# Cumulative sums of dt in a Mamba-2 block on TensorE: eight fp32 products per block of 512 tokens made three, with another layout of the transposed sums

## The reference, cut to what matters

```python
dt = softplus(zxbcdt[..., -NHEADS:] + dt_bias)      # 16 heads
A = -exp(A_log)
dA = exp(dt * A)
def step(state, inp):                               # over the tokens
    state = state * dA_t[:, :, None, None] + (dt_t[:, :, None] * x_t)[..., None] * B_t[:, None, None, :]
    y = einsum('bhpn,bn->bhp', state, C_t)
```

## Time and profile before

| | |
|---|---|
| Median of three runs | 3551.24 us (3545.0 to 3558.86) |
| Span of the profiled execution, the only time that the profile gives for it | 3539.0 us |
| TensorE busy (matmul) | 3336.7 us, 94% |
| VectorE, ScalarE, GpSimd busy | 77%, 73%, 51% |
| Mean granted TensorE clock | 0.978 of full speed |
| TensorE's share of the chain that ended last | 74% |

### The profile page before, as it was taken

The page is one execution under the profiler, slowest core; times in us unless marked ns, Lnnn a source line. Parts: engine busy times, 40 slices in busy tenths (PEclk is TensorE's granted clock), DMA queues, the critical chain, the costliest instruction groups (busy, mean ns, idle before and its releaser), DMA issues.

```text
span 3539.0 us, 64210 instructions
## 1 busy us (share of the span) xinstructions
PE 3336.7 (94%) x24314; PEld 1934.5 (55%) x24314; DVE 2723.3 (77%) x4854; ACT 2574.7 (73%) x4690; POOL 1810.1 (51%) x1355
## 2 busy tenths in 40 slices
PE   6899999999999999999868999999999999999998
PEld 4455555555555555555434555555555555555554
DVE  6798878887779787889977677777777777777764
ACT  6888888888888888887637566677666766666664
POOL 1333333333333342333547887876665765566665
PEclk9899999999999999999878999999999999999999
DMA  5355544365544355445468576777776776767664
GB/s 164 93 117 117 122 96 104 100 126 117 123 100 107 93 123 115 125 99 87 84 121 174 97 129 110 134 147 147 126 136 119 152 134 121 120 129 133 120 113 67
DMA packets 809428, 419.43 MB, mean 119 GB/s; under 512 B 566583, under 2 KB 733879, under 8 KB 807072
## 3 DMA queue, kind: packets, MB, share of 16 engines
q1 hardware_dynamic: 752800, 312.58, 43.4%
q0 software_dynamic: 56320, 102.75, 16.0%
HBM read 176.00 MB, written 101.71 MB: 78 GB/s over the span
## 4 chain that ended last, share of the span: by engine, by line
PE 74%; DVE 7%; DMA 7%; ACT 4%; POOL 3%; issue 3%; SPq 1%; ACTq 0%; DVEq 0%; POOLq 0%
PE pair L1314 9%; PE pair L1362 8%; PE pair L1236 8%; PE pair L1471 8%; PE pair L1284 7%; PE pair L1324 5%; PE pair L1378 4%; PE pair L1393 4%; DMA yT<-yhl 3%; PE pair L1439 3%; PE pair L1440 3%; PE pair L1304 2%; PE pair L1409 2%; PE pair L1295 2%; PE pair L1457 1%
## 5 line engine op out<-in xcount | busy, mean ns | idle before, releaser
L1619 DVE SCALAR_TENSOR_TENSOR cv<-raw,taps,cv 128x512 f32<-128x512 f32 x480 | 429.3, 909 | 42.9 <-ACT cv L2013 38.2
L1864 DVE TENSOR_REDUCE smx<-pair 128x2 f32<-128x514 f32 x512 | 349.3, 685 | 66.3 <-PE pair L1409 66.1
L1236 PE MATMUL pair<-xhT,whi 128*128 128x512 f16 x1280 | 382.5, 381 | 2.7 <-DVE state L1674 1.0
L2284 POOL TENSOR_TENSOR ph<-pf,ph 128x1024 f16<-128x1024 f32 x128 | 291.9, 2281 | 180.1 <-ACT ph L2149 179.6
L1314 PE MATMUL pair<-ohi,yT 128*128 128x512 f16 x1024 | 325.0, 390 | 30.6 <-DMA yT<-yhl 30.6
L2143 ACT ACTIVATE pf<-pair 128x1024 f32<-128x1024 f32 x256 | 261.8, 1023 | 106.6 <-PE pair L1440 94.1
L1284 PE MATMUL pair<-zhi,xhT 128*128 128x512 f16 x1024 | 326.3, 380 | 1.8 <-ACT zs L2055 1.2
L2043 ACT ACTIVATE de<-de,cum 128x128 f32<-128x128 f32 x1024 | 308.4, 388 | 0.3
L2289 POOL TENSOR_TENSOR ohl<-of,ohl 128x256 f16<-128x256 f32 x256 | 216.5, 851 | 110.7 <-ACT ohl L2156 109.2
L2149 ACT CAST ph<-pf 128x1024 f16<-128x1024 f32 x256 | 267.0, 1043 | 4.6 <-PE pair L1459 0.2
L2257 POOL DMA_INDIRECT gat<-rows,slot_i x192 | 195.7, 1019 | 108.3 <-DVE slot_i L1812 74.4
(11 more groups left out here) (267 smaller groups left out, 9969.2 us busy)
## 6 DMA issues: line engine op xcount, KB each, us to landing
de<-cum SPq DMA_DIRECT2D x64, 1024.0 KB, 9.4
rows<-rowt SPq DMA_DIRECT2D x16, 1040.0 KB, 6.5
xin<-x SPq DMA_DIRECT2D x16, 1024.0 KB, 8.9
y<-xin SPq DMA_DIRECT2D x16, 1024.0 KB, 5.2
y<-ob POOLq DMA_DIRECT2D x64, 256.0 KB, 6.3
qb<-qa SPq DMA_DIRECT2D x32, 512.0 KB, 4.4
rbc<-rank SPq DMA_DIRECT2D x63, 256.0 KB, 4.1
wst<-wkv SPq DMA_DIRECT2D x32, 256.0 KB, 4.0
```

Source lines behind the costliest of these rows:

```text
L1236: ins = pe.matmul(bk[:], w[:, k, ws], xt[:, ha, k, :], start=n == 0, stop=n == 3 * KD - 1)
L1619: ve.scalar_tensor_tensor(c_[:], r_[:, t:t + BLK], taps[:, ct, t:t + 1], c_[:], ALU.mult, ALU.add).then_inc(done, 1)
L1864: ve.tensor_reduce(smx[:, qt, 2 * h2:2 * h2 + 2], sc[:, :, 0:NK + 1], AX.X, ALU.max)
L2284: po.tensor_tensor(p_[:, 1], f[:], p_[:, 0], ALU.subtract).then_inc(S.plp, 1)
```

## The change

`cum` gets three products in place of eight. The first takes all 64 columns of the block at once (weights `upper`, 64 moving columns, 128x64 result). The transposed ones are two products of 32 weight columns each (two chunks by 16 heads), with results in partitions 0 to 31 and 32 to 63, which are different column parts of the array. The transposed sums are thus 64 partitions (chunk, head) by 128 tokens, and no longer 16 by 512. ScalarE copies 64x128, `cum_store` writes 64 rows of 128 numbers, and the DRAM buffer has the layout (block, chunk and head, token). A chunk's 2048 numbers then lie together, and `bc_in` reads them as one run for each partition. `cumT` keeps its bytes in SBUF. In the planner the cost of `cum` goes from 1.9 to 0.6 us, and that of `cum_exp` from 0.9 to 0.6 us.

```diff
@@ arrange_steps
         elif name == "cum":
-            add("PE", 1.9, step, [("dt", a)], [("single", [("cum_copy", a)]), ("single", [("cum_exp", a)])])
+            add("PE", 0.6, step, [("dt", a)], [("single", [("cum_copy", a)]), ("single", [("cum_exp", a)])])
...
-        add("ACT", 0.9, ("cum_exp", i), [("cum_copy", i)] + [last(("y_in", CK * (i - 2) + CK - 1)), last(("cum_store", i - 1))])
+        add("ACT", 0.6, ("cum_exp", i), [("cum_copy", i)] + [last(("y_in", CK * (i - 2) + CK - 1)), last(("cum_store", i - 1))])
@@ make_plan, turns
         yield ("cum", i)
-        yield 1.9
+        yield 0.6
@@ program
-        cum_d = scratch("cum", (NBLK, NH, BLK), F32)
+        cum_d = scratch("cum", (NBLK, CK * NH, P), F32)
...
-            cumT = sb(mam, "cumT", [NH, BLK], F32)
+            cumT = sb(mam, "cumT", [CK * NH, BLK], F32)[:, 0:P]
@@ tensor_engine, cum
-                xr = dts[:, 0, :].rearrange("p (c h) -> p c h", c=CK)
+                xr = dts[:, 0, :]
                 q.wait_ge(S.da, i + 1)
                 wait_given_back(q, "cum", i)
-                bk = bank("cum", i)
-                for c in range(CK):
-                    ins = pe.matmul(bk[:, c * NH:(c + 1) * NH], upper, xr[:, c, :], start=True, stop=True)
-                ins.then_inc(S.cum_mm, 1)
+                pe.matmul(bank("cum", i)[:, 0:CK * NH], upper, xr, start=True, stop=True).then_inc(S.cum_mm, 1)
                 wait_given_back(q, "cum", i, n=1)
-                bk = bank("cum", i, n=1)
-                for c in range(CK):
-                    ins = pe.matmul(bk[0:NH, c * P:(c + 1) * P], xr[:, c, :], upper, start=True, stop=True)
+                bk, half = bank("cum", i, n=1), CK * NH // 2
+                for a in range(2):
+                    ins = pe.matmul(bk[a * half:(a + 1) * half, 0:P], xr[:, a * half:(a + 1) * half], upper, start=True, stop=True)
                 ins.then_inc(S.cumT_mm, 1)
@@ scalar_engine, cum
-                ac.copy(cumT[:], bank("cum", i, n=1)[0:NH, :]).then_inc(S.cumT, 1)
+                ac.copy(cumT, bank("cum", i, n=1)[0:CK * NH, 0:P]).then_inc(S.cumT, 1)
@@ sync_engine, cum_store and bc_in
-                sp.dma_start(cum_d[i], cumT[:]).then_inc(S.cum_out, 16)
+                sp.dma_start(cum_d[i], cumT).then_inc(S.cum_out, 16)
...
-                sp.dma_start(de[ch % 2][:], cum_d[i][:, c * P:(c + 1) * P].partition_broadcast(P)).then_inc(S.bc[ch % 2], 16)
+                sp.dma_start(de[ch % 2][:].rearrange("p h t -> p (h t)"), cum_d[i][c * NH:(c + 1) * NH, :].rearrange("h t -> (h t)").partition_broadcast(P)).then_inc(S.bc[ch % 2], 16)
```

## The result

The changed kernel takes 3515.89 us (median of four runs, 3514.2 to 3522.4) beside 3549.95 us of the kernel before (3545.0 to 3558.86). The ratio is 0.9909, with a 95% interval of 0.9889 to 0.9929: faster by 34 us, where the prediction said 16 and a range down to 3519. In a second comparison the ratio was 0.9915 (0.9891 to 0.9939). One execution of a later kernel (new_first), of 12169.3 us, counts as slow and is in no ratio.

The account below looks back on a forecast made before the run. TensorE's own work was taken to bound the Mamba stage's middle. Cum steps 14.8 + 0.5, less 1.5 for stalls, plus 2.0 for transfers gave 15.8 us off 3551.2: 3535 us, own range 3529 to 3543, overall 3519 to 3557.

Parts of the forecast that it names:

- The bound: Mamba stage, 200 to 1600 us: TensorE, 98.7% busy, sets the length of 14 of the 16 blocks.
- 1.5 us set aside for new stalls: TensorE in the Mamba stage: part of the gain turns into stalls, 1.5 us subtracted.
- TensorE's part: Cum steps on TensorE: 0.81 us in place of 1.87, 1.06 us saved; 14.8 us over fourteen, 0.5 for the last.
- the bound for products side by side: Cum step: if the two transposed products run side by side, 0.59 us remain and 1.28 us are saved.
- The upper bound for drains: Cum step: if each of two width changes waits for a matmul to come out, 0.16 us twice added, 0.74 saved.
- The transfers: cum_store and the load of de: load lands in 7 us in place of 9.4; all together 0 to 6 us, taken 2.
- the first gate: yT's issue at 132.82 us, held behind a load of de: a load 2.4 us shorter gives about 2 us there.
- The tail's stalls: Tail of the Mamba stage: three waits behind transfers sum to 14.9 us; gain 0 to 2.4 us, taken as 0.
- The slower case: Rival, 3566 us, chance 0.10: new planner costs reorder SP and VectorE, one more stall before proj in each of 14 blocks.
- the median's 12.2 us over the span: Whole run: median 3551.2 us against span 3539.0, put down to start and end left out and the runs' spread.
- The case of more than the sum: Rival, 3524 us, chance 0.22: products side by side 18.6 us, yT stalls halved 6, first gate 2; 27 us.

Follow-up runs that it names:

- new_first: The kernel before with the new DRAM layout for block 0 alone, in a second buffer; blocks 1 to 15 keep the old layout: ratio 0.9954.
- work_only: The changed kernel with the planner's three old costs put back, so new products and layout in the order of before: ratio 0.9913 to before.
- work_again: work_only once more, unaltered, on the same chip as the repeat of the changed kernel: ratio 0.9906 to before.
- layout_only: The kernel before with the new DRAM layout alone (loads of de in 8 KB runs), old products, costs and order: ratio 0.9945.
- Order-only: The kernel before with only the planner's three costs of the change, so another order of steps, same products and transfers: ratio 1.0052.

## Why the prediction was wrong

**The bound: right.** TensorE sets the middle of the Mamba stage, and what was freed stayed freed (98.9% busy). The 1.5 us set aside for new stalls were not lost in the changed kernel, whose stalls shrank; in work_only and work_again they grew to 18.4 and 13.5 us and the gain was the same. One row was misread, without effect on the sum: from 1700 us VectorE is busy 88.42 of 110 us, which is 80% and not 88%.

**TensorE's part: right in kind, 19% small.** I took 0.81 us for the step (1.06 saved) and had 0.59 as the bound for products side by side. It is 0.61 us (1.26 saved). My 0.81 is what the step takes on one column part (0.82), so the sum of passes and pauses was right for that case, and the value chosen was the wrong end. Over 14.5 steps that is 18.3 in place of 15.4 us. The upper bound for drains (1.13 us) did not occur.

**The transfers: the step that failed.** The sum gave the shorter load of `de` 2 us, within 0 to 6, at the first gate, and the forecast's own range of 3529 to 3543 did not even use the 6. Alone the layout is worth 0.55%, measured three times (0.9945, 0.9943, 0.9946), some 19 us. Three readings failed. The landing was taken as 7 us and is 4.8: 5.2 was a bound from another transfer of 1 MB, and the truth lies beyond it. Its users were sought among those that wait for `de` (2.8 us), while the loss was with what stood behind it on SP: a transposing DMA whose issue ends only when the copies before it have landed, and loads of x and rows that landed 4 us later. I had seen this in the earlier trace rows and counted the one place. And even that place was counted by the wait alone: it brought 6.4 us in layout_only's profile and not 2, since the 24 products behind the wait had run in 8.09 us in place of 5.35, at the lower clock. No term of the sum was for the clock, though by the estimate above it is some 4 to 6 of the layout's 19 us. How the others divide between the start and later gates stays open. The tail's stalls were set to zero rightly: layout_only has 14.7 us of them, from 1675 to 1800 us, where before has 14.9:

```profile
PE pair L1314 <- DMA yT<-yhl: 14.7, 3, 7.3
```

**The order: a rival that was real and was hidden.** The slower case said that the planner's costs would move gates behind other transfers. Order-only shows it, +0.52%, with `proj` stalls of 16.8 us for 12.1. It fell short of the 31 us priced, about half of it came with a lower granted clock (0.9770 for 0.9797), and with the new load and products nothing of it is left (change 0.9915, work_again 0.9906). The load takes the stalls away (16.8 to 3.0 us). Why the whole change in the new order is as good as in the old, though the order by itself costs some 18 us, stays open.

**The time itself.** The forecast subtracted 15.8 us from the median and put the median's 12.2 us over the span down to what the span leaves out and to the spread of executions. The first is 1.3 us; the rest is the spread, which goes with the granted clock. That by itself changed no term, but it made the profile's difference (17.9 us) agree with the forecast by chance. The case of more than the sum (3524, at 0.22), with products side by side and relieved gates, had most of the mechanisms and still gave the load too little.

## What to carry to other kernels

Cost a transfer by what is queued behind it and not only by who reads its result: on a queue shared with transposing DMAs, a copy of twice the time can hold the turn behind it, and a stall that it causes can cost TensorE its clock on top. Look at the granted clock of each kernel beside its ratio. When a planner orders the work, measure a change once with the old order held, as here with the costs put back; else its effect and the order's, of about the same size, are read as one. And compare executions, not single profiles, for a change under one per cent.

## What the runs showed of the hardware that was not expected

- 1 MB broadcast from DRAM to 128 partitions lands in 9.4 us as runs of 512 bytes and in 4.8 us as runs of 8 KB. The Trainium skill (DMA: Bandwidth & Descriptors, Specifications) gives 512 bytes as the least transfer for full rate; these two figures do not agree, and the measurement decides for this pattern.
- On SP the issue of a transposing DMA lasts until the copies issued before it have landed: 8.67 us behind a `de` issued 0.4 us earlier in before, 7.95 in order_only, both ending within 0.3 us of the landing of `de`; its median is 1.93 us.
- After TensorE's wait of 3.6 us at the first gate, 24 products took 8.09 us, and 5.35 us where it had not waited. The executions of a kernel differ by some 4 us for each 0.001 of the mean granted clock (an estimate from the sets of before).
- A source of 16 contiguous rows of 512 bytes is moved in the same 8 KB runs whether or not the program joins the dimensions (687,316 packets).
- Over its passes of 0.11 us, a cum step takes 0.11 us if its transposed products have 16 weight columns (1.87 us, 16 passes), 0.16 with 32 on one column part (0.82, 6 passes) and 0.19 with 64 (0.63, 4 passes). That this is the price of changing the width is not shown. The first product's two passes of 64 moving columns take 0.26 us, where 16 columns took 0.22 for two.
- ScalarE's copy of 64x128 takes 0.242 us, the same as its 128x64 (0.240), and not the 0.29 expected of twice the elements per partition.
- The same attention program takes 1721 and 1738 us in two profiles, and the Mamba stage before it ends at 1790.6 and 1781.1 us.
